# Alternating the products of two score or value blocks in a decoder layer's attention

## Chip, cores and metric

The kernel runs on one core of one Trainium2 chip. The metric is the device time of one execution in microseconds (us); 0.2% of it is 5 us.

## The reference, cut to what matters

One decoder layer on x (2 batches, 512 tokens, 1024 features), float32:

```python
q = (x @ w_q)   # 32 heads of 128;  k, v = x @ w_k, x @ w_v   # 8 heads of 128
lq = x @ w_lq   # 256 wide;  lk = lq @ w_lk, lv = x @ w_lv    # 32 heads of 128
q, k, lk = rope(q), rope(k), rope(lk)
attn = causal_attn(q, k, v);  lat = causal_attn(q, lk, lv)
x = layernorm(x + attn @ w_o + lat @ w_lo)
x = layernorm(x + fake_quant(x) @ fake_quant(ctx))
x = layernorm(x + fp8_simulated(x) @ weight)
```

causal_attn is softmax(mask(q k^T / sqrt(128))) v.

## The kernel before, in words

**Split products.** Every float32 operand of a large product is split into a high part and a low part, both fp32r. `product` (L1198) makes one product of three matmuls into the same PSUM tile: high by high (L1200), high by the moving low part (L1201), low by high (L1202). The first name is the stationary operand, which a weight load puts into the array before each matmul; the profile lists these loads as engine PEld, with the same line as their matmul.

**Groups.** For each of 2 batches there are 8 groups, one per key and value head, so 16 in all. A group G computes, in this order on TensorE: lk from lq, the values of the group before's last unit, k and v, q, lv (each from weight chunks of 128x512 that SP loads, ScalarE copies to w_hi at L478 and GpSimd turns into w_lo at L414), and then 8 units of attention: 4 query heads with k, v and the same 4 with lk, lv. lv lands in the four banks BANK_B; ScalarE copies each to lv_hi (L658), VectorE subtracts to lv_lo (L962) and counts `lv_lo_done`.

**A unit** has three steps on TensorE. `scores(G, u)` (L1211) makes the lower triangle of the 512x512 scores in four blocks, one per tile of 128 queries, with 512, 384, 128 and 256 keys, in the order of the table `TRI`; they lie in banks 0, 1, 1 and 2. Each block is one `product`, and counts `scores_ready`. VectorE's `mask_scores` (L801, its instructions at L809) masks the blocks and takes a row minimum in the order of `TRI`; it waits for 1, 3, 3 and 4 counts. ScalarE makes exponentials (L515), VectorE normalises (L816, L820). `transposes(G, u)` (L1235, L1248) waits for the masks of unit u + 1 and for the normalised rows of unit u, and transposes ten 128x128 tiles into banks 0 to 2. ScalarE copies them to pT_hi (L521), VectorE makes pT_lo (L826). `values(G, u)` (L1253) multiplies by v or lv in four blocks by key tile, 512, 384, 256 and 128 queries wide (`sorted(PT)`), all accumulated in bank 3 (columns 128*kt to 512), and counts `o_ready`. ScalarE and VectorE take it to o_hi (L525) and o_lo (L831).

**Order around it.** The order is written out by hand (L1435 to L1447): part 0, scores 0, part 1, scores 1, and then for each u: part, transposes u, part, values u, scores u + 2. A part is one chunk of the output projection, 12 matmuls 512 wide, added up by VectorE at L845. In a steady group part(0) lies between the lv products and scores 0; in the first group of batch 0 there is nothing there.

At unit 0, `scores` waits for lv_lo before it overwrites the banks: the block in bank 0 for the first lv_lo of the group, the one in bank 1 for the second, the one in bank 2 for the third. Everything else that scores and values wait for is waited for once, ahead of their first matmul.

Of the kernel before, what the change touches and what calls it, by code (L numbers as in the profile page):

```python
# [14 lines left out]
P = 128  # L15
B, S, D = 2, 512, 1024
H, KVH, HD = 32, 8, 128
# [5 lines left out]
TT = S // P  # L23
N = 512
# [30 lines left out]
TRI = [(3, 0, 0, 512), (2, 1, 512, 384), (0, 1, 896, 128), (1, 2, 1024, 256)]  # L55
PT = [(0, 0, 0, 512), (1, 1, 512, 384), (3, 1, 896, 128), (2, 2, 1024, 256)]
SPW = 1280
PT_BANKS = [(0, 0, 512), (1, 512, 512), (2, 1024, 256)]


# [35 lines left out]
def program(nc, wstream, xt, x, ctxt, wf, cos, sin, mask, ident, quant, out):  # L96
    ctx = ExitStack()
    with ctx:
        def sem(name):
            return ctx.enter_context(nc.semaphore(name))  # L100
# [11 lines left out]
        def sb(name, shape, dt, stack=ctx):  # L112
            return stack.enter_context(nc.sbuf_tensor(name, shape, dt))
# [19 lines left out]
        with ExitStack() as mem:  # L133
            xT_hi, xT_lo = (sb(n, [P, KT, S], F32R, mem) for n in ("xT_hi", "xT_lo"))
            lq_hi, lq_lo = (sb(n, [P, 2, S], F32R, mem) for n in ("lq_hi", "lq_lo"))
            k_hi, k_lo = (sb(n, [P, S], F32R, mem) for n in ("k_hi", "k_lo"))
            v_hi, v_lo = (sb(n, [P, TT, HD], F32R, mem) for n in ("v_hi", "v_lo"))
            q_hi, q_lo = (sb(n, [P, HG, S], F32R, mem) for n in ("q_hi", "q_lo"))
            lk_hi, lk_lo = (sb(n, [P, HG, S], F32R, mem) for n in ("lk_hi", "lk_lo"))
            lv_hi, lv_lo = (sb(n, [P, TT, HG * HD], F32R, mem) for n in ("lv_hi", "lv_lo"))  # L140
            probs = sb("probs", [P, 2, SPW], F32, mem)
            pT_hi, pT_lo = (sb(n, [P, SPW], F32R, mem) for n in ("pT_hi", "pT_lo"))
            acc = sb("acc", [P, TT, D], F32, mem)
# [51 lines left out]
        BANK_B = [ctx.enter_context(nc.psum_tensor(f"bank_b{i}", [P, N], F32)) for i in range(4)]  # L195
# [22 lines left out]
        lv_hi_done, lv_lo_done = sem("lv_hi_done"), sem("lv_lo_done")  # L218
        scores_ready = sem("scores_ready")
# [249 lines left out]
        def _(act):  # L469
# [48 lines left out]
            def pT_high(G, u):  # L518
                for i, (bank, at, w) in enumerate(PT_BANKS):
                    act.wait_ge(pT_ready, 3 * (UNITS * G + u) + i + 1)  # L520
                    nc.scalar.activation(pT_hi[:, at:at + w], BANK_B[bank][:, 0:w], ACT.Copy).then_inc(pT_hi_done, 1)  # L521
# [260 lines left out]
        def _(dve):  # L782
# [40 lines left out]
            def pT_low(G, u):  # L823
                for i, (bank, at, w) in enumerate(PT_BANKS):
                    dve.wait_ge(pT_hi_done, 3 * (UNITS * G + u) + i + 1)
                    nc.vector.tensor_tensor(pT_lo[:, at:at + w], BANK_B[bank][:, 0:w],  # L826
                                            pT_hi[:, at:at + w].bitcast(F32), ALU.subtract).then_inc(pT_lo_done, 1)
# [368 lines left out]
        def _(pe):  # L1196
            def product(dst, still, move, start, stop):


                nc.tensor.matmul(dst, still[0], move[0], start=start, stop=False)  # L1200
                nc.tensor.matmul(dst, still[0], move[1], start=False, stop=False)  # L1201
                return nc.tensor.matmul(dst, still[1], move[0], start=False, stop=stop)  # L1202

            def weights(pos, a, z):
                s = SPLIT_SLOT[pos]
                return w_hi[:, s, a:z], w_lo[:, s, a:z]

            def xk(k, a=0, z=S):
                return xT_hi[:, k, a:z], xT_lo[:, k, a:z]

            def scores(G, u):  # L1211

                h = 2 * (u // 4) + u % 2
                if u == 0:

                    pe.wait_ge(rope_lo, ROPES * G + ROPES)
                elif u == 1:

                    pe.wait_ge(masked, 4 * (UNITS * G + 1))
                else:  # L1220

                    pe.wait_ge(pT_lo_done, 3 * (UNITS * G + u - 1))
                for i, (qt, bank, at, w) in enumerate(TRI):
                    q = q_hi[:, h, P * qt:P * qt + P], q_lo[:, h, P * qt:P * qt + P]
                    if u % 4 < 2:
                        k = k_hi[:, 0:w], k_lo[:, 0:w]
                    else:
                        k = lk_hi[:, h, 0:w], lk_lo[:, h, 0:w]
                    col = at - N * bank
                    if u == 0 and i != 2:  # L1230

                        pe.wait_ge(lv_lo_done, TT * G + bank + 1)
                    product(BANK_B[bank][:, col:col + w], q, k, True, True).then_inc(scores_ready, 1)

            def transposes(G, u):  # L1235

# [16 lines left out]
            def values(G, u):  # L1253

                h = 2 * (u // 4) + u % 2
                pe.wait_ge(pT_lo_done, 3 * (UNITS * G + u + 1))
                if u == 0:

                    pe.wait_ge(v_lo_done, G + 1)
                    pe.wait_ge(lv_lo_done, TT * G + TT)  # L1260
                else:

                    pe.wait_ge(o_lo_done, UNITS * G + u)
                for kt, _, at, w in sorted(PT):
                    if u % 4 < 2:
                        v = v_hi[:, kt], v_lo[:, kt]
                    else:
                        v = lv_hi[:, kt, HD * h:HD * (h + 1)], lv_lo[:, kt, HD * h:HD * (h + 1)]
                    p = pT_hi[:, at:at + w], pT_lo[:, at:at + w]
                    last = product(BANK_B[3][:, P * kt:N], v, p, kt == 0, kt == TT - 1)  # L1270
                last.then_inc(o_ready, 1)

            def split(b, g, c):
# [56 lines left out]
            def group(b, g, first):  # L1330
# [15 lines left out]
                if not first:  # L1346

                    values(G - 1, UNITS - 1)
# [85 lines left out]

                part(0)  # L1435
                scores(G, 0)
                part(1)
                scores(G, 1)
                for u in range(UNITS):
                    if u < UNITS - 1:  # L1440
                        part(2 * u + 2)
                    transposes(G, u)
                    if u < UNITS - 1:
                        part(2 * u + 3)
                        values(G, u)
                    if u + 2 < UNITS:
                        scores(G, u + 2)  # L1447
# [6 lines left out]
            for b in range(B):  # L1454

                for c in range(C_LQ):
                    split(b, 0, c - C_LQ)
                    for k in (2 * c, 2 * c + 1):
# [3 lines left out]
                        for l in range(2):  # L1462
                            if k == 0 and b:

                                pe.wait_ge(added, 4 * (4 * KVH * b - 1) + l + 1)
                            at = LAT * (k % 2) + P * l
                            last = product(BANK_A[l][:], weights(LQ_POS + c, at, at + P), xk(k),
                                           k == 0, k == KT - 1)
# [13 lines left out]
                for i in range(C_TAIL // 2):  # L1482
                    if i == 2:
                        values(KVH * (b + 1) - 1, UNITS - 1)
                    if i in (0, 3):

                        pe.wait_ge(o_lo_done, UNITS * KVH * (b + 1) - (0 if i else 1))
                    last_output(b, i)
# [155 lines left out]
```

## Time and profile before

| | |
|---|---|
| median of 3 runs | 2533.32 us (2532.18 to 2535.01) |
| profiled execution, own time | 2531.58 us |
| its span | 2529.6 us |
| TensorE busy | 2468.4 us, 98% of the span |
| matmuls, weight loads | 12456 and 12456 |
| VectorE, ScalarE, GpSimd busy | 69%, 45%, 36% |
| mean granted clock | 0.994 |

PE is TensorE's matmuls, PEld its weight loads, DVE VectorE, ACT ScalarE, POOL GpSimd. The span is shorter than the execution's own time by what lies around the program. Matmuls are pipelined, so the duration of one is longer than the distance to the next.

### The profile page before, as it was taken

Reading aid. Unit: us, or ns where it says so; the run is one execution under the profiler, and the core shown is the slowest. Engines: PE = TensorE matmul, PEld = TensorE weight load, DVE = VectorE, ACT = ScalarE, POOL = GpSimd, SP = SyncE. Lnnn points to the kernel's source line nnn. Section 1 sums busy time; section 2 is a strip of 40 time slices with the busy share of each in tenths; the row PEclk is TensorE's granted clock in tenths of the full one; section 3 lists DMA queues with packets and bytes.
Section 4 is the critical chain, followed back from the end, with each engine's and each line's share of the span. In section 5 each row is a group of like instructions: output and inputs, shape, how many; then the busy total and the mean of one; then the engine's idle time right before and its main releaser. Section 6 shows DMA issues by size and latency. Waiting matters only on the chain.

```text
span 2529.6 us, 40729 instructions
## 1 busy us (share of the span) xinstructions
PE 2468.4 (98%) x12456; PEld 2088.7 (83%) x12456; DVE 1734.9 (69%) x3589; ACT 1131.9 (45%) x2576; POOL 921.8 (36%) x696
## 2 busy tenths in 40 slices
PE   7899999999999999999989999999999999999998
PEld 6688888888888888887767888888888888888877
DVE  5676767767676767665587676767767677667656
ACT  3444434344444535444365453544444354544551
POOL 4334242433434242432543424243342524334210
PEclk9999999999999999999999999999999999999999
DMA  5323231312223232322423323222232323234411
GB/s 179 89 80 92 64 104 58 98 56 75 87 75 95 62 98 60 90 64 87 136 89 131 105 70 109 69 85 77 83 104 71 109 70 106 60 90 147 154 34 67
DMA packets 124407, 226.26 MB, mean 89 GB/s; under 512 B 13088, under 2 KB 21408, under 8 KB 124192
## 3 DMA queue, kind: packets, MB, share of 16 engines
q1 hardware_dynamic: 119552, 216.91, 28.2%
q10 hardware_dynamic: 4768, 8.39, 0.9%
q8 instruction: 30, 0.49, 0.1%
q14 instruction: 57, 0.47, 0.1%
HBM read 206.37 MB, written 18.87 MB: 89 GB/s over the span
## 4 chain that ended last, share of the span: by engine, by line
PE 94%; DVE 3%; issue 1%; ACT 1%; DMA 0%; POOL 0%; SPq 0%; PEldq 0%; ACTq 0%; DVEq 0%
PE bank_a L1200 16%; PE bank_a L1202 16%; PE bank_a L1201 16%; PE bank_b L1200 13%; PE bank_b L1201 13%; PE bank_b L1202 13%; PE bank_b L1248 5%; PE bank_b L1517 1%; PE bank_a L1325 0%; DMA probs<-xt 0%; DVE probs L809 0%; PE bank_b L1384 0%; PE bank_b L1500 0%; POOL w_lo L414 0%; DVE acc L845 0%
## 5 line engine op out<-in xcount | busy, mean ns | idle before, releaser
L414 POOL TENSOR_TENSOR w_lo<-w_raw,w_hi 128x512 fp32r<-128x512 f32 x632 | 844.0, 1344 | 1419.2 <-ACT w_hi L478 1411.2
L478 ACT ACTIVATE w_hi<-w_raw 128x512 fp32r<-128x512 f32 x632 | 392.9, 626 | 287.9 <-DMA w_raw<-wstream 141.5
L1200 PE MATMUL bank_a<-w_hi,o_hi 128*128 128x512 f32 x1024 | 410.7, 401 | 9.0 <-DVE acc L845 4.8
L1202 PE MATMUL bank_a<-w_hi,o_lo 128*128 128x512 f32 x1024 | 403.5, 394 | 0.0
L1201 PE MATMUL bank_a<-w_lo,o_hi 128*128 128x512 f32 x1024 | 403.1, 394 | 0.0
L826 DVE TENSOR_TENSOR pT_lo<-bank_b,pT_hi 128x512 fp32r<-128x512 f32 (+1 forms) x384 | 207.0, 594 | 267.1 <-ACT pT_hi L521 267.1
L515 ACT ACTIVATE probs<-probs,row_min 128x512 f32<-128x512 f32 (+3 forms) x512 | 281.6, 552 | 240.8 <-DVE row_min L809 238.4
L525 ACT ACTIVATE o_hi<-bank_b 128x512 fp32r<-128x512 f32 x128 | 76.8, 600 | 455.4 <-PE bank_b L1202 455.4
L820 DVE TENSOR_SCALAR probs<-probs,row_inv 128x512 f32<-128x512 f32 (+3 forms) x512 | 261.4, 570 | 4.5
L1200 PEld LDWEIGHTS bank_a<-w_hi,o_hi 128*128 128x128 f32 x1024 | 193.5, 189 | 44.3 <-issue 7.8
L1200 PE MATMUL bank_a<-xT_hi,w_hi 128*128 128x512 f32 x544 | 214.2, 394 | 14.4 <-POOL w_lo L414 14.4
L1202 PEld LDWEIGHTS bank_a<-w_hi,o_lo 128*128 128x128 f32 x1024 | 193.1, 189 | 41.7
L1201 PEld LDWEIGHTS bank_a<-w_lo,o_hi 128*128 128x128 f32 x1024 | 193.6, 189 | 34.9
L809 DVE CUSTOM_DVE_ANT_0 probs<-bank_b,mask_sb 128x512 f32<-128x512 f32 (+3 forms) x512 | 220.5, 482 | 2.4 <-PE bank_b L1202 1.0
L1202 PE MATMUL bank_a<-xT_hi,w_lo 128*128 128x512 f32 x544 | 212.8, 391 | 0.0
L1201 PE MATMUL bank_a<-xT_lo,w_hi 128*128 128x512 f32 x544 | 212.7, 391 | 0.0
L1200 PE MATMUL bank_b<-w_hi,xT_hi 128*128 128x512 f32 x512 | 199.2, 389 | 0.0
L1201 PE MATMUL bank_b<-w_lo,xT_hi 128*128 128x512 f32 x512 | 199.2, 389 | 0.0
L1202 PE MATMUL bank_b<-w_hi,xT_lo 128*128 128x512 f32 x512 | 199.2, 389 | 0.0
L790 DVE TENSOR_TENSOR probs<-bank_a,cos_sb 128x512 f32<-128x512 f32 x128 | 88.2, 689 | 136.5 <-PE bank_a L1202 130.5
L521 ACT ACTIVATE pT_hi<-bank_b 128x512 fp32r<-128x512 f32 (+1 forms) x384 | 171.6, 518 | 18.1 <-PE bank_b L1248 18.1
L1248 PE MATMUL bank_b<-ident_sb,probs 128*128 128x128 f32 x1280 | 162.3, 274 | 11.7 <-DVE row_min L809 10.9
(176 smaller groups left out, 4785.4 us busy)
## 6 DMA issues: line engine op xcount, KB each, us to landing
w_raw<-wstream SPq DMA_DIRECT2D x632, 256.0 KB, 2.7
stage<-ctx SPq DMA_DIRECT2D x32, 256.0 KB, 2.7
stage_w<-wf SPq DMA_DIRECT2D x32, 256.0 KB, 2.8
q_scratch<-stage_q SPq DMA_DIRECT2D x32, 128.0 KB, 2.3
wf_hi_scratch<-piece_hi SPq DMA_DIRECT2D x16, 256.0 KB, 3.0
wf_lo_scratch<-stage_w SPq DMA_DIRECT2D x16, 256.0 KB, 3.3
wf_hi<-wf_hi_scratch SPq DMA_DIRECT2D x8, 512.0 KB, 7.9
wf_lo<-wf_lo_scratch SPq DMA_DIRECT2D x8, 512.0 KB, 11.8
```

The costliest lines, as they stand in the source:

```text
L414: nc.gpsimd.tensor_tensor(w_lo[:, s], w_raw[:, r], w_hi[:, s].bitcast(F32), ALU.subtract).then_inc(lo_done, 1)
L478: nc.scalar.activation(w_hi[:, s], w_raw[:, r], ACT.Copy).then_inc(hi_done, 1)
L515: nc.scalar.activation(part, part, ACT.Exp, bias=row_min[:, u % 2, i:i + 1], scale=-1.0, accum_out=row_sum[:, u % 2, i:i + 1]).then_inc(ex ...
L521: nc.scalar.activation(pT_hi[:, at:at + w], BANK_B[bank][:, 0:w], ACT.Copy).then_inc(pT_hi_done, 1)
L790: nc.vector.tensor_tensor(a, bank[:], cos_sb[:], ALU.mult)
L809: nc.vector.tensor_tensor_reduce(out=probs[:, u % 2, at:at + w], in0=BANK_B[bank][:, col:col + w], in1=mask_sb[:, N - w:N], scale=-SCALE, ...
L820: nc.vector.tensor_scalar(part, part, row_inv[:, u % 2, i:i + 1], None, ALU.mult).then_inc(normed, 1)
L826: nc.vector.tensor_tensor(pT_lo[:, at:at + w], BANK_B[bank][:, 0:w], pT_hi[:, at:at + w].bitcast(F32), ALU.subtract).then_inc(pT_lo_done, 1)
L1200: nc.tensor.matmul(dst, still[0], move[0], start=start, stop=False)
L1201: nc.tensor.matmul(dst, still[0], move[1], start=False, stop=False)
L1202: return nc.tensor.matmul(dst, still[1], move[0], start=False, stop=stop)
L1248: last = nc.tensor.transpose(BANK_B[bank][:, dst:dst + P], probs[:, u % 2, src:src + P], ident_sb[:])
```

## The change

The blocks of scores and values are taken in two pairs: the first table row with the third, the second with the fourth. In both tables these are 512 with 128 columns, and 384 with 256. Within a pair the loops run over the three parts of the product outside and the two blocks inside. The operands, the sums and the number of matmuls stay. Scores of unit 0 wait once per pair for the lv_lo of the pair's second block; values start their accumulation at block 0, part 0, and end it with the last part of the last block.

```diff
+TRI_PAIRS = [(0, 2), (1, 3)]
+PT_PAIRS = [(0, 2), (1, 3)]
...
-                for i, (qt, bank, at, w) in enumerate(TRI):
-                    q = q_hi[:, h, P * qt:P * qt + P], q_lo[:, h, P * qt:P * qt + P]
-                    if u % 4 < 2:
-                        k = k_hi[:, 0:w], k_lo[:, 0:w]
-                    else:
-                        k = lk_hi[:, h, 0:w], lk_lo[:, h, 0:w]
-                    col = at - N * bank
-                    if u == 0 and i != 2:
-
-                        pe.wait_ge(lv_lo_done, TT * G + bank + 1)
-                    product(BANK_B[bank][:, col:col + w], q, k, True, True).then_inc(scores_ready, 1)
+                for pair in TRI_PAIRS:
+                    if u == 0:
+
+                        pe.wait_ge(lv_lo_done, TT * G + TRI[pair[1]][1] + 1)
+                    for part in range(3):
+                        for i in pair:
+                            qt, bank, at, w = TRI[i]
+                            q = (q_lo if part == 2 else q_hi)[:, h, P * qt:P * qt + P]
+                            if u % 4 < 2:
+                                k = (k_lo if part == 1 else k_hi)[:, 0:w]
+                            else:
+                                k = (lk_lo if part == 1 else lk_hi)[:, h, 0:w]
+                            col = at - N * bank
+                            last = nc.tensor.matmul(BANK_B[bank][:, col:col + w], q, k, start=part == 0, stop=part == 2)
+                            if part == 2:
+                                last.then_inc(scores_ready, 1)
...
-                for kt, _, at, w in sorted(PT):
-                    if u % 4 < 2:
-                        v = v_hi[:, kt], v_lo[:, kt]
-                    else:
-                        v = lv_hi[:, kt, HD * h:HD * (h + 1)], lv_lo[:, kt, HD * h:HD * (h + 1)]
-                    p = pT_hi[:, at:at + w], pT_lo[:, at:at + w]
-                    last = product(BANK_B[3][:, P * kt:N], v, p, kt == 0, kt == TT - 1)
+                for pair in PT_PAIRS:
+                    for part in range(3):
+                        for i in pair:
+                            kt, _, at, w = PT[i]
+                            if u % 4 < 2:
+                                v = (v_lo if part == 2 else v_hi)[:, kt]
+                            else:
+                                v = (lv_lo if part == 2 else lv_hi)[:, kt, HD * h:HD * (h + 1)]
+                            p = (pT_lo if part == 1 else pT_hi)[:, at:at + w]
+                            first, stop = (kt, part) == (0, 0), (pair, part, i) == (PT_PAIRS[-1], 2, pair[1])
+                            last = nc.tensor.matmul(BANK_B[3][:, P * kt:N], v, p, start=first, stop=stop)
                 last.then_inc(o_ready, 1)
```

## Rows read from the trace of the kernel before

**Rows 1.** The page: busy time, and the chain that ended last, by engine.
```profile
PE 2468.4 (98%) x12456; PEld 2088.7 (83%) x12456; DVE 1734.9 (69%) x3589; ACT 1131.9 (45%) x2576; POOL 921.8 (36%) x696
...
PE 94%; DVE 3%; issue 1%; ACT 1%; DMA 0%; POOL 0%; SPq 0%; PEldq 0%; ACTq 0%; DVEq 0%
```
**Rows 2.** Stretch table of one steady group: busy us, granted clock, DMA share, GB/s.
```profile
960.14:1103.85 143.71, 143.71 (x734) 122.97 (x733) 99.94 (x210) 64.42 (x153) 52.83 (x40) 1.00 0.27 79
```
**Rows 3.** Waits of TensorE, whole span: total us, times, longest us.
```profile
PE bank_b L1200 <- DVE lv_lo L962: 6.5, 1, 6.5
```
**Rows 4.** Timeline of loads and one matmul, values then scores: start us, duration us.
```profile
1005.54 0.19 PEld L1201 LDWEIGHTS bank_b<-pT_lo,v_hi 128*128 128x128 f32 x1
...
1005.54 0.39 PE L1200 MATMUL bank_b<-pT_hi,v_hi 128*128 128x512 f32 x1
...
1005.77 0.19 PEld L1202 LDWEIGHTS bank_b<-pT_hi,v_lo 128*128 128x128 f32 x1
...
1006.22 0.19 PEld L1201 LDWEIGHTS bank_b<-pT_lo,v_hi 128*128 128x128 f32 x1
...
1007.12 0.19 PEld L1201 LDWEIGHTS bank_b<-pT_lo,v_hi 128*128 128x128 f32 x1
1007.22 0.19 PEld L1202 LDWEIGHTS bank_b<-pT_hi,v_lo 128*128 128x128 f32 x1
...
1007.45 0.19 PEld L1201 LDWEIGHTS bank_b<-lk_lo,q_hi 128*128 128x128 f32 x1
...
1008.14 0.19 PEld L1201 LDWEIGHTS bank_b<-lk_lo,q_hi 128*128 128x128 f32 x1
...
1008.49 0.19 PEld L1200 LDWEIGHTS bank_b<-lk_hi,q_hi 128*128 128x128 f32 x1
1008.66 0.19 PEld L1201 LDWEIGHTS bank_b<-lk_lo,q_hi 128*128 128x128 f32 x1
1008.77 0.19 PEld L1202 LDWEIGHTS bank_b<-lk_hi,q_lo 128*128 128x128 f32 x1
...
1009.00 0.19 PEld L1201 LDWEIGHTS bank_b<-lk_lo,q_hi 128*128 128x128 f32 x1
...
1009.36 0.19 PEld L1201 LDWEIGHTS bank_a<-w_lo,o_hi 128*128 128x128 f32 x1
```
**Rows 5.** Matmuls by form, 970 to 1028 us: busy us, mean ns of one.
```profile
L1200 PE MATMUL bank_b<-pT_hi,v_hi 128*128 128x512 f32 x3 | 1.2, 389 | 0.0
...
L1202 PE MATMUL bank_b<-pT_hi,v_lo 128*128 128x384 f32 x3 | 1.0, 339 | 0.0
...
L1200 PE MATMUL bank_b<-pT_hi,v_hi 128*128 128x256 f32 x3 | 0.9, 290 | 0.0
...
L1201 PE MATMUL bank_b<-pT_lo,v_hi 128*128 128x256 f32 x3 | 0.8, 282 | 0.0
...
L1200 PE MATMUL bank_b<-pT_hi,v_hi 128*128 128x128 f32 x3 | 0.7, 220 | 0.0
```
**Rows 6.** Timeline where scores of unit 0 begin: a steady group, then group 0.
```profile
1093.02 2.48 DVE L962 TENSOR_TENSOR lv_lo<-bank_b,lv_hi 128x512 fp32r<-128x512 f32 x4 [6.50 <-ACT lv_hi L658]
...
1094.17 0.19 PEld L1200 LDWEIGHTS bank_b<-k_hi,q_hi 128*128 128x128 f32 x1
...
87.90 2.48 DVE L962 TENSOR_TENSOR lv_lo<-bank_b,lv_hi 128x512 fp32r<-128x512 f32 x4 [6.05 <-ACT lv_hi L658]
88.71 0.19 PEld L1200 LDWEIGHTS bank_b<-k_hi,q_hi 128*128 128x128 f32 x1 [2.48 <-issue]
```
**Rows 7.** Timeline: last mask row of a unit, and the transposes that wait for it.
```profile
1011.19 0.08 DVE L809 DVE_READ_ACCUMULATOR2_ANT row_min<- 128x1 f32 x1
...
1012.11 0.27 PE L1248 MATMUL bank_b<-ident_sb,probs 128*128 128x128 f32 x1
...
1102.58 0.07 DVE L809 DVE_READ_ACCUMULATOR2_ANT row_min<- 128x1 f32 x1
...
1103.69 0.38 PE L1248 MATMUL bank_b<-ident_sb,probs 128*128 128x128 f32 x2
```

## The prediction

> **What bounds the kernel now.** I read the page's first part and the chain that ended last: TensorE is busy for 98% of the span, holds 94% of the chain, at nearly full granted clock [rows 1]. The stretch table of one steady group, of which 14 of the 16 are alike, shows TensorE busy for all of its 143.71 us at a granted clock of 1.00, 2.4 GHz, with VectorE at 99.94 us [rows 2]. The waits of TensorE, third, are single events in the first group of a batch: the one of this change's place is 6.5 us, once [rows 3]. So whatever changes the time between two matmuls is paid in full, and what shifts on other engines is paid only once a wait appears.
>
> The fourth view, the weight loads in order of time, prices a matmul [rows 4]. A load starts when the matmul before it starts to stream: the load and the matmul of 1005.54 have one start. So the gap between two loads is what one matmul costs. 512 columns cost 0.23 us (1005.54 to 1005.77), 384 cost 0.17 (1008.14 to 1008.66 for three), 256 cost 0.12 (1009.00 to 1009.36), and 128 cost 0.11: the three narrow ones of the values stream from 1007.12 and the next 512 from 1007.45. Durations are finer [rows 5]: a 512 lasts 389 ns and costs 227, so I take 162 off a duration (my choice of constant) where the matmul waited for no load. The first narrow one of the values streams in 220 - 162 = 58 ns, yet the next one starts 0.11 later. A narrow product is bound by the load that follows it.
>
> **The change part by part.** Its intent can only be to hide that load: 110 - 58 = 52 ns for each of 3 narrow products, in 128 scores and 128 values.
>
> First, *the alternation itself*. Which matmul has the long gap? The load for the second narrow product of the scores starts at 1008.66, when the first one starts to stream, though the 384 before it streams from 1008.49 and the load during that one began at 1008.49 too; the load after it comes 0.11 later (1008.77), which is all that a load needs [rows 4]. Had a second load been allowed to run ahead, it would have begun about 1008.60. It didn't, and the wide rows say the same: 0.23 between loads that need 0.11. One load runs ahead, never two. Then in 512, 128, 512 the load of the second 512 can only start as the 128 starts, and the 512 waits for it: 0.23 + 0.11, as now. Each pair costs what its members cost apart; the narrow matmul merely has another neighbour. Number of loads and matmuls: unchanged. Taken: 0. That product now gives q_hi or v_hi twice running is no credit lost either: loads are issued again for each of the three parts [rows 4], and the second matmul of a product, with the same stationary operand, has its load at 1005.54 like any other.
>
> The Trainium skill ("TensorE: Matmul & The Clock Gate", section "Step-by-step: what each phase is for") says that TensorE's 64-deep window pulls weight loads ahead of matmuls in flight when they go to the background buffer. Read as many loads ahead, it would give the first rival below; the trace agrees only with one load ahead.
>
> Second, *changes of width*. They carry small surcharges [rows 5]. The last 384 lasts 339 ns and the 256 after it 290, so 177 + 128 = 305 ns for a 384 with a 256 behind it; a 256 behind a 256 costs 282 - 162 = 120. The new order has such a pair three times: 915 ns. The values take 0.90 us for these six (1006.22 to 1007.12), the scores 0.52 for the 384s and 0.36 for the 256s, 0.88 [rows 4]. That is 15 + 35 = 50 ns a unit. For the 512 and 128 pairs the rows show 0.23 and 0.11 whatever stands before (1007.45 follows a narrow one by 0.11), taken as 0. So 50 x 128 units = 6.4 us. Bounds: below, every surcharge vanishes, 3 x 227 + 520 + 3 x 120 + 330 = 1891 ns against 1.91 us, in values (1005.54 to 1007.45) and in scores (1007.45 to 1009.36), 0.02 x 256 sets = -5.1 us. Above, width changes within a set go from 3 to 11, and each of the 8 more costs the 8 ns by which 290 lies over 282: 64 x 256 = +16.4 us. Whether the surcharge stays when the order alternates no row shows; I take the pair that exists.
>
> Third, *the earlier wait at unit 0*. Before, the first scores product waits for the first lv_lo and the second for the second; now the pair waits for the second at once. VectorE's four lv_lo of a steady group run from 1093.02 for 2.48 us, 0.62 each: the first two end at 1093.64 and 1094.26. The first scores load starts at 1094.17 [rows 6]. In group 0 the load started at 88.71 after the first lv_lo, which by the same count ended at 88.52: 0.19 later. So in the changed kernel the load starts at 1094.45, and streaming follows 0.11 behind, as behind every load that is waited for, at 1094.56. Now it follows a load that was early, with the end of the 512 before it, 0.23 behind the load, at 1094.40. The difference is 0.16 us, and the bound TensorE doesn't get it back. 14 x 0.16 = 2.2 us. In the first group of each batch TensorE already waits for the first lv_lo (load at 88.71, and the 6.5 us of the second batch) [rows 3, 6], so it waits one lv_lo longer, 0.6 each: 1.2 us. Bounds: 0 if the release is quicker and the two late ones absorb theirs, 4 us if the later masks of the two first groups add up. The third lv_lo, at 1094.9, is there before the second pair's loads near 1095.5: no cost.
>
> Fourth, *later readiness of the scores*. The first tile is ready after 5 matmuls instead of 3, at 0.9 instead of 0.7 us from the start; the second mask, which waits for three, can go after 11 instead of 9, about 0.25 later. In the unit loop VectorE ends the masks of the scores of 1007.45 at 1011.27, and the transposes that need them start at 1012.11 [rows 7]: slack 0.84 us, over three times the delay. Behind unit 0 the masks may end 0.45 later; those of unit 1, out at 1102.65, are then out near 1103.1, against transposes at 1103.69 [rows 7]. Queued behind a late mask are the exponentials and, behind them on ScalarE, a w_hi made four chunks ahead. Cost 0; if the cover is gone, whatever exceeds it, once per unit. No DMA, no instruction of SP or POOL moves.
>
> **Sum.** 0 + 6.4 + 2.2 + 1.2 = +9.8 us on the profiled execution's 2531.58 us (span 2529.6 and 2 around it): 2541.4. The median of the runs shown is 1.7 above that execution; on it the forecast is 2543.1.
>
> **Rivals.**
> *Two or more loads run ahead.* Then a wide matmul of 227 ns nearly hides the load of both neighbours (two loads, 220), a narrow one costs about 58, and 52 x 768 = 39.9 us are saved, less 3.4 of waiting: about 2496.8. For it: only that loads are separate instructions that overlap matmuls. Against: every load start in rows 4. This is the case on the other side.
> *No surcharge.* The alternating order costs no more than blocks do, or a little less; the waits remain. -2 to +5 us, about 2535, no change that shows. For it: the 282 and 290 differ for no reason that I can give, so it may be a phase and not a price.
> *The masks become the wait.* If the masks ended over 0.84 us later, TensorE would stand before the transposes in each. At 0.2 us beyond the slack, 0.2 x 128 = 26 us more: about 2568. Against: I count 0.25.
> *The change doesn't alternate.* Were the matmuls issued in another order than written, nothing would move but the waits. They follow the code's order in every row I read; I give this nothing of its own.
>
> **Chances.** Forecast 0.58; no surcharge 0.30; two loads ahead 0.07; masks 0.05. About 0.2%, 5 us, is what a measurement of this kernel can tell from no change. The forecast's spread reaches from +5 to +19, so nearly all of it is slower; a little falls inside, and of the no-surcharge case all but a sliver is inside. Faster 0.08, same 0.32, slower 0.60. The range takes the low ends together, -5.1 + 1.8 if the waits are absorbed in part, to 2530, and the high ends, 16.4 + 4 = 20.4, less a little because both at their worst is unlikely, to 2552; the two outer rivals are left out, with 0.12, and a little for what I haven't seen.
>
> **What would show it.** Right: after each 128 the next load starts 0.11 behind the load before, and a 512 behind it starts to stream only then; a set of 12 takes 1.92 to 1.94 us; the first scores product of a steady group starts at 0.1 to 0.2 us of idle after lv_lo; TensorE's counts stay at 12456. Wrong: load starts 0.06 apart anywhere in the pairs (two ahead), a set near 1.75 us; or waits of the transposes for the masks in the unit loop; or a 256 behind a 384 that lasts 282 ns, which takes the surcharge away.

## The result, and the profile after

The changed kernel takes 2538.72 us (median of 15 runs, 2536.42 to 2541.33) against 2533.15 us beside it: a ratio of 1.0021, 95% interval 1.0013 to 1.0028, which is +5.3 us with +3.3 to +7.1. Forecast were +9.8 us, between 2530 and 2552. The direction and the range held; the sum was nearly twice too large, and its two leading terms were sized wrong in the same direction. A piece that no term named, the clock, fills part of the gap, so that the number came as near as it did is in part luck.

The stretch table of one steady group of the changed kernel, to be read beside [rows 2]:

```profile
962.86:1106.71 143.85, 143.85 (x735) 122.67 (x734) 100.15 (x210) 64.48 (x152) 52.81 (x40) 1.00 0.28 79
```

A group grows from 143.71 to 143.85 us (143.82 to 143.87 in all but one of the 48 distances read). TensorE is still busy throughout: what is lost lies inside the matmuls' distances. The twelve distances from one steady group's first lk product to the next one's, six in each batch, sum to 1724.6 us before (mean of three profiles) and 1726.1 after (mean of four): +1.5 us, or some 1.7 for all 14 steady groups.

The weight loads in order of time, for the values and scores that answer to [rows 4]. A row "x2" holds the loads of one part of a pair, and its start is that of the first. In these rows the stationary operand, the one that is loaded, is the second name behind the arrow:

```profile
1008.52 0.30 PEld L1282 LDWEIGHTS bank_b<-pT_lo,v_hi 128*128 128x128 f32 x2
1008.86 0.30 PEld L1282 LDWEIGHTS bank_b<-pT_hi,v_lo 128*128 128x128 f32 x2
1009.20 0.30 PEld L1282 LDWEIGHTS bank_b<-pT_hi,v_hi 128*128 128x128 f32 x2
1009.49 0.31 PEld L1282 LDWEIGHTS bank_b<-pT_lo,v_hi 128*128 128x128 f32 x2
1009.78 0.30 PEld L1282 LDWEIGHTS bank_b<-pT_hi,v_lo 128*128 128x128 f32 x2
1010.08 0.30 PEld L1239 LDWEIGHTS bank_b<-lk_hi,q_hi 128*128 128x128 f32 x2
1010.43 0.30 PEld L1239 LDWEIGHTS bank_b<-lk_lo,q_hi 128*128 128x128 f32 x2
```

A pair of 512 and 128 takes 0.34 us (1008.52 to 1008.86): 0.23 + 0.11, the sum of what the two cost apart. A pair of 384 and 256 takes 0.29. Nothing was hidden. The durations say where the wait went. The forms of the matmuls, mean ns of one, for [rows 5]:

```profile
L1282 PE MATMUL bank_b<-pT_lo,v_hi 128*128 128x512 f32 x3 | 1.3, 445 | 0.0
...
L1282 PE MATMUL bank_b<-pT_hi,v_lo 128*128 128x384 f32 x3 | 1.0, 340 | 0.0
...
L1282 PE MATMUL bank_b<-pT_lo,v_hi 128*128 128x256 f32 x3 | 0.8, 278 | 0.0
...
L1282 PE MATMUL bank_b<-pT_lo,v_hi 128*128 128x128 f32 x3 | 0.7, 222 | 0.0
```

In the kernel before, the second and third narrow matmul of a set lasted about 275 ns, waiting some 55 ns of it for their own load:

```profile
L1201 PE MATMUL bank_b<-pT_lo,v_hi 128*128 128x128 f32 x3 | 0.8, 276 | 0.0
```

Now each lasts 222, and the 512 behind it lasts 445 instead of 389: the same wait, moved to the neighbour. A reader who looked at the narrow rows alone would see a gain of a fifth.

The earlier wait of unit 0, first in a steady group (for [rows 6]), then the whole span's row for [rows 3]:

```profile
1095.73 2.48 DVE L965 TENSOR_TENSOR lv_lo<-bank_b,lv_hi 128x512 fp32r<-128x512 f32 x4 [6.50 <-ACT lv_hi L661]
...
1097.07 0.30 PEld L1239 LDWEIGHTS bank_b<-k_hi,q_hi 128*128 128x128 f32 x2 [0.23 <-DVE lv_lo L965]
```
```profile
PE bank_b L1239 <- DVE lv_lo L965: 9.7, 2, 7.0
```

The first scores load now waits for the second lv_lo. It starts 1.34 us after the first lv_lo began, where it started 1.15 after (1093.02 to 1094.17). In the first group of a batch the matmul's wait is 7.0 instead of 6.5 us, and there are two such groups in the list instead of one.

The piece that no term named is the clock. Around the tail, rows of the stretch table (after PE, PEld, DVE, ACT and POOL comes the granted clock), the kernel before first, then the changed one:

```profile
2424.00:2428.00 4.00, 1.76 (x19) 1.21 (x18) 3.97 (x5) 3.30 (x6) 2.17 (x1) 1.00 0.00 0
2428.00:2432.00 4.00, 4.00 (x19) 3.25 (x19) 3.72 (x4) 3.97 (x6) 2.60 (x2) 1.00 0.00 0
```
```profile
2431.00:2434.00 3.00, 0.76 (x14) 0.59 (x12) 2.96 (x4) 2.48 (x5) 1.85 (x1) 1.00 0.00 0
2434.00:2438.00 4.00, 4.00 (x15) 3.19 (x13) 3.90 (x4) 4.00 (x4) 2.89 (x2) 0.57 0.00 0
```

TensorE sits idle for over 2 us in both. In the kernel before it goes on at 2.4 GHz (granted 1.00); in the changed one the next stretch is granted 0.57, mostly 1.2 GHz, and issues 15 matmuls in place of 19. From the last group's lk products to the end the changed kernel takes 292.9 us instead of 291.1: 1.8 us, of which the steady group in it makes about 0.1 and the clock 1.6 to 1.7.

### The profile page after: what moved, and what is told of

The parts are those of the page before. It is cut to its first block, busy times and chain, and to the rows that moved or that the text cites. A ratio compares the mean times of both kernels' runs of the same rounds, so it can differ in the third digit from the quotient of the medians.

```text
span 2537.5 us, 40715 instructions
## 1 busy us (share of the span) xinstructions
PE 2472.9 (97%) x12456; PEld 2085.4 (82%) x12456; DVE 1736.9 (68%) x3589; ACT 1132.1 (45%) x2576; POOL 923.0 (36%) x696
## 4 chain that ended last, share of the span: by engine, by line
PE 94%; DVE 3%; issue 2%; ACT 1%; DMA 0%; POOL 0%; SPq 0%; PEldq 0%; ACTq 0%; DVEq 0%; POOLq 0%
PE bank_a L1203 16%; PE bank_a L1204 16%; PE bank_a L1205 16%; PE bank_b L1282 10%; PE bank_b L1239 9%; PE bank_b L1204 7%; PE bank_b L1203 7%; PE bank_b L1205 7%; PE bank_b L1256 5%; PE bank_a L1337 1%; PE bank_b L1529 1%; POOL w_lo L417 0%; DVE probs L812 0%; DMA probs<-xt 0%; PE bank_b L1396 0%
## 5 line engine op out<-in xcount | busy, mean ns | idle before, releaser
L1256 PE MATMUL bank_b<-ident_sb,probs 128*128 128x128 f32 x1280 | 161.7, 273 | 12.6 <-DVE row_min L812 11.8
## 6 DMA issues: line engine op xcount, KB each, us to landing
wf_lo<-wf_lo_scratch SPq DMA_DIRECT2D x8, 512.0 KB, 11.8
```

Source lines behind the costliest of these rows:

```text
L1256: last = nc.tensor.transpose(BANK_B[bank][:, dst:dst + P], probs[:, u % 2, src:src + P], ident_sb[:])
```

## The experiments

All ratios are against the kernel before, run in turn on the same chip.

**Theory.** One load runs ahead, so alternation is neutral but for some ns; the loss comes from the earlier wait. **Rivals.** The alternation costs it; or loads run further ahead and something else eats the gain.

**e1: the wait alone**

```diff
-                        pe.wait_ge(lv_lo_done, TT * G + bank + 1)
+                        pe.wait_ge(lv_lo_done, TT * G + max(bank, 1) + 1)
```

> The kernel before, with only the wait moved: scores of unit 0 wait for the second lv_lo ahead of the first block. No alternation. My theory (waits and the rest of the scores order are separate costs): the first scores load of a steady group starts 0.11 to 0.12 us after the second lv_lo ends, streaming 0.14 us later than before, 14 x 0.14 = 2.0 us, and 0.6 us in each first group: +3.2 us. Rival (the cost of the change is in the alternation): 0 to +1 us.

Measured 1.0015 (1.0006 to 1.0024), +3.8 us, interval +1.5 to +6.1. So the wait alone makes a loss, by the middle value most of it. But its steady groups grow less than expected:

```profile
741.60:885.40 143.80, 143.80 (x736) 122.89 (x733) 100.27 (x211) 64.30 (x152) 52.37 (x40) 1.00 0.26 79
```

0.09 a group, 1.3 us in all, and the scores of each first group start 0.6 later: 2.5. In its profile the tail has the slow clock too, worth 1.7, though nothing alternates:

```profile
2428.00:2432.00 4.00, 4.00 (x16) 3.21 (x14) 3.90 (x4) 3.99 (x4) 2.95 (x2) 0.57 0.00 0
```

**e2: both alternations, with the waits put back**

```diff
-                    if u == 0:
-                        pe.wait_ge(lv_lo_done, TT * G + TRI[pair[1]][1] + 1)
                     for part in range(3):
                         for i in pair:
                             qt, bank, at, w = TRI[i]
+                            if u == 0 and part == 0 and i != 1:
+                                pe.wait_ge(lv_lo_done, TT * G + bank + 1)
```

> The changed kernel with the waits of the kernel before put back: the first matmul waits for the first lv_lo, the narrow one behind it for the second, the last block for the third. My theory: the narrow product's load in a steady group waits 0.04 us instead of 0.14, so 1.4 us of the 2.0 come back and up to 0.2 in each first group: 1.5 to 2.5 us less than the changed kernel, about +3 us against before. Rival (alternation costs it all): still +5 us.

Measured 1.0013 (1.0004 to 1.0022), +3.3 us. Steady group and the first group's start behave as expected: the group takes 143.74 us, 0.03 over the kernel before, and the first group's scores start when they did.

```profile
740.76:884.50 143.74, 143.74 (x734) 122.72 (x733) 100.22 (x212) 64.30 (x152) 52.37 (x40) 1.00 0.26 79
```

The tail's clock stays up (291.3 us from the last group's lk to the end). The total agrees with the number expected, but its interval reaches from +1.0 to +5.6 and doesn't exclude the rival, so the group time is the evidence here, not the total. Of the +3.3 only 0.4 to 0.5 lies in the steady groups. Its profile has another fall of the clock, near 1210 us, worth 1.6 (see e9 to e12); what is left isn't placed.

**e3 and e4: one alternation each.** e3 has the scores of the changed kernel and the values of the kernel before, e4 the reverse:

```diff
-                for pair in PT_PAIRS:
...
+                for kt, _, at, w in sorted(PT):
...
```
```diff
-                for kt, _, at, w in sorted(PT):
...
+                for pair in PT_PAIRS:
...
```

> Only the scores alternate, with the change's wait. From the loads of the changed kernel: a set of scores takes 1920 ns instead of 1913, so 128 x 7 ns = +0.9 us, and the waits +3.2: about +4.1 us. Rival (values carry the loss): under +2 us.

> Only the values alternate. A set of values takes 1903 ns instead of 1904 in the changed kernel: 0 us, within the noise, though its 512s cost 7 ns more each and its 256s 8 ns less. My prediction's surcharge of 15 ns a set would give +1.9 us; the rival that a second load runs ahead would give -20 us.

e3: 1.0023 (1.0014 to 1.0032), +5.8 us, where +4.1 was expected: that number left out the tail's fall, which e3's profile has. e4: 0.9999 (0.999 to 1.0008), no change. Steady groups, e3 then e4:

```profile
741.39:885.22 143.83, 143.83 (x734) 122.72 (x733) 100.34 (x212) 64.29 (x152) 52.38 (x40) 1.00 0.27 79
```
```profile
739.93:883.59 143.66, 143.66 (x734) 122.88 (x733) 100.17 (x212) 64.32 (x152) 52.46 (x40) 1.00 0.26 79
```

e3 over e1 is the scores' alternation without the wait: 0.03 a group. e4 under the kernel before is the values': -0.05 a group. Added up they would give 14 x (0.03 - 0.05) = -0.3 us. Both together, read directly as the changed kernel over e1, which has the same wait, give 1726.1 against 1725.8 us over the twelve distances: +0.03 a group, +0.4 us in all. Either way alternation costs next to nothing in the steady groups, where I had 6.4.

**e5: a larger dose of the wait**

```diff
-                        pe.wait_ge(lv_lo_done, TT * G + bank + 1)
+                        pe.wait_ge(lv_lo_done, TT * G + TT)
```

> The kernel before, with every block of unit 0 waiting for the fourth lv_lo: a larger dose of the wait. In a steady group the fourth ends 1.34 us after the first load's time; with 0.11 to the load and 0.11 to streaming less the 0.23 that the load was ahead: +1.33 us x 14 = 18.7 us, and 1.8 us in each first group: +22 us. Rival (the wait is absorbed behind it): clearly less, under +10 us.

Measured 1.0089 (1.0075 to 1.0103), +22.5 us, and a group of 145.00 with 1.00 us of TensorE idle:

```profile
893.90:1038.90 145.00, 144.00 (x736) 122.89 (x733) 100.02 (x211) 64.41 (x152) 52.76 (x40) 1.00 0.26 78
```

1.29 a group: a steady group pays the wait in full.

**e6: narrow matmuls halved in the changed order**

```diff
+                            n = w if w > P else w // 2
-                            last = nc.tensor.matmul(BANK_B[bank][:, col:col + w], q, k, ...
+                            last = nc.tensor.matmul(BANK_B[bank][:, col:col + n], q, k[:, 0:n], ...
```

and the same in values.

> The changed kernel with every 128-wide matmul of scores and values cut to 64 columns; half of the diagonal block of the first 128 queries and of the last key block is left out of the computation. My theory (a narrow matmul is bound by the load behind it, which needs 0.11 us, whatever its neighbours): no change against the changed kernel, +5 us against before, load gaps still 108 ns. Rival (alternation has hidden the load and narrow matmuls cost their streaming): 768 x 27 ns = 20 us less.

Measured 1.0005 (0.9996 to 1.0014), +1.3 us: 4 us under the changed kernel, not 0, but far from 20. By form:

```profile
L1284 PE MATMUL bank_b<-pT_lo,v_hi 128*128 128x512 f32 x4 | 1.9, 476 | 0.0
...
L1284 PE MATMUL bank_b<-pT_lo,v_hi 128*128 128x64 f32 x4 | 0.8, 193 | 0.0
```
```profile
1006.23 0.30 PEld L1284 LDWEIGHTS bank_b<-pT_lo,v_hi 128*128 128x128 f32 x2
1006.57 0.30 PEld L1284 LDWEIGHTS bank_b<-pT_hi,v_lo 128*128 128x128 f32 x2
1006.91 0.30 PEld L1284 LDWEIGHTS bank_b<-pT_hi,v_hi 128*128 128x128 f32 x2
```

The narrow matmul is 29 ns shorter and the 512 behind it 31 ns longer; the pair still takes 0.34 us. This puts the rival of a hidden load out: even with half its columns gone a narrow product costs the 0.11 of the load behind it, next to the widest block. Of the 4 us, 1.6 are the tail's clock, which stays up here (291.3 us to the end), and about 1.2 smaller distances elsewhere in the sets (groups of 143.74). The last us I can't place; it is less than the interval.

e6 shows that the columns don't set the 0.11, but not yet that the load does: every matmul here has a load, so a fixed price per matmul would look alike. e5's trace settles that. There TensorE has been idle for 1.00 us when the scores of unit 0 begin:

```profile
960.16 0.19 PEld L1200 LDWEIGHTS bank_b<-k_hi,q_hi 128*128 128x128 f32 x1 [1.43 <-DVE lv_lo L962]
960.16 0.50 PE L1200 MATMUL bank_b<-k_hi,q_hi 128*128 128x512 f32 x1 [1.00 <-DVE lv_lo L962]
960.27 0.19 PEld L1201 LDWEIGHTS bank_b<-k_lo,q_hi 128*128 128x128 f32 x1
```

With no matmul ahead of it, the first load still takes 0.108 to 0.109 us until the next one starts, in all 14 steady groups, and its matmul lasts 0.50 us, 0.11 more than the 0.39 of a 512 that waits for nothing. The load alone needs the 0.11. It isn't the price of every load: the bf16 loads of the kernel before, 0.10 us long, come 0.055 us apart (seven of them end 0.43 us after the first one's start).

```profile
2440.69 0.43 PEld L1312 LDWEIGHTS bank_b<-ident_b,q 128*128 128x128 bf16 x7
```

**e7: other partners, values only**

```diff
-PT_PAIRS = [(0, 2), (1, 3)]
+PT_PAIRS = [(0, 3), (1, 2)]
```

> Only the values alternate, with other partners: 512 with 256, and 384 with 128. My theory (a pair costs what its members cost apart, plus some ns of surcharge): within 1 us of e4, sets of 1.90 us; the 128 costs 0.108 behind a 384 as behind a 512. Rival (what matters is that the widest covers the narrowest): slower than e4 by 2 us or more.

Measured 1.0009 (1.0 to 1.0018), +2.3 us, with groups of 143.81 against e4's 143.66:

```profile
740.86:884.67 143.81, 143.81 (x734) 122.97 (x733) 99.94 (x212) 64.39 (x152) 52.83 (x40) 1.00 0.27 79
```

My number missed, and the rival's fits. Its mechanism doesn't: the 128s last 221 to 222 ns, and the 384s behind them 391 to 397 instead of 339, the same transfer of the wait as behind a 512. What differs are some ns elsewhere: here a 512 behind a 256 lasts 395 to 403.

```profile
L1276 PE MATMUL bank_b<-pT_hi,v_lo 128*128 128x512 f32 x4 | 1.6, 403 | 0.0
L1276 PE MATMUL bank_b<-pT_lo,v_hi 128*128 128x384 f32 x4 | 1.6, 397 | 0.0
...
L1276 PE MATMUL bank_b<-pT_hi,v_hi 128*128 128x128 f32 x4 | 0.9, 222 | 0.0
```

So such surcharges are real, 0.15 us a group or 18 ns a unit, but I can't tell their sign from the neighbours' widths. More than half of them even lies in the scores, whose order e7 leaves as it was: their 384 with k_lo or lk_lo lasts 342 to 346 ns instead of 337 to 338. The total isn't evidence for the rival either: e4 and e7 ran beside different runs of the kernel before, and e7's profile has the fall near 1210 us, worth 1.6, that e4's hasn't.

**e8: the change again**, beside e5 to e7.

> The changed kernel as it is, beside these on one chip. Expected +5.3 us as measured, 3 to 7; of it the waits make about 3 and the sets 0.7.

Measured 1.0021 (1.0012 to 1.003), +5.3 us, as before.

**e9 to e12: is the clock's fall one of the kernel or of the execution?** Both kernels unchanged, twice each.

> The kernel before, unchanged, profiled again. In its first profile the clock stayed at 2.4 GHz near 1210 us and near 2430 us; in the changed kernel's two profiles there is a stretch of 3.4 us at 1.2 GHz at each, worth 1.6 and 1.7 us. Theory A (the clock's falls there differ from execution to execution and belong to no kernel): this profile or the next shows at least one such stretch. Theory B (they belong to the shifted waits of the changed kernel): neither shows one.

> As the run before it: the kernel before, unchanged. Theory A: its pattern of half-clock stretches differs from the other profiles of the same kernel. Theory B: it is the first profile's pattern, none near 1210 and 2430 us.

> The changed kernel, unchanged, profiled again. Theory A: at least one of the two stretches at 1.2 GHz (near 1212 and 2430 us) is missing here or in the next run. Theory B: both are there in both runs, as in its two profiles so far.

> As the run before it: the changed kernel, unchanged. In every profile of it the steady groups are expected at 143.82 to 143.86 us, the set of scores at 1920 ns and the set of values at 1903 ns, whatever the clock does in the stretches between.

The two places answer differently. Near 1210 us, in the second batch's lq products, the fall is in one of three profiles of the kernel before and in all four of the changed one; a fall there is worth 1.6 us (15.6 instead of 14.0 from the first lq product to lk). Of the other kernels' profiles, one each, e2, e3, e5, e6 and e7 have it, e1 and e4 don't. e10 has it:

```profile
1211.00:1215.00 4.00, 4.00 (x12) 3.14 (x11) 0.00 (x0) 1.04 (x2) 4.00 (x4) 0.57 0.78 234
2428.00:2432.00 4.00, 1.76 (x19) 1.33 (x18) 3.93 (x5) 3.30 (x6) 2.37 (x1) 1.00 0.00 0
2432.00:2436.00 4.00, 4.00 (x19) 3.28 (x18) 3.47 (x3) 3.96 (x6) 2.41 (x1) 1.00 0.00 0
```

In the tail it is in none of the three before, and in all four after, as e12 shows:

```profile
2432.00:2436.00 4.00, 4.00 (x17) 3.22 (x15) 3.90 (x4) 3.97 (x5) 2.98 (x2) 0.57 0.00 0
```

So theory A holds near 1210, where it can happen to either kernel, and B as far as seven profiles can say for the tail. Of the other kernels, by one profile each, the tail's fall is in e1 and e3, not in e2, e4, e5, e6 and e7. e6 has the changed order and the pair's wait and doesn't show it; e5 has the longest wait and doesn't either. The idle ahead of it, 2.46 us between the starts of two matmuls, is the same in all. So no single edit brings it; that small shifts in time decide it is my guess, and how they would I leave open.

The mean granted clocks of all executions bear on this as well. They are 0.9937 and 0.9936 in the kernel before (33 and 27 executions) and 0.9928 and 0.9927 in the changed one (15 and 11): 0.0009 less, which over 2535 us is about 2 us of lost work if it all fell into TensorE's working time. So the changed kernel loses more to the clock in its other executions too. In e1 the mean over 11 executions is 0.9936, as before; that the tail's fall is part of e1's +3.8 rests on its one profile.

The steady groups repeat as e12's expectation says: 143.83 to 143.86 in it.

## Why the prediction was right, and where it was not

*The alternation hides nothing* (taken: 0). Right, and shown by the loads of the changed kernel and by e6: one load runs ahead, and a load for the matmul after a narrow one starts only with the narrow one. The rival of two or more loads ahead is out: 0.34 us a pair, where it needed 0.29 or less (227 + 58 ns). The Trainium skill's sentence in "TensorE: Matmul & The Clock Gate" ("Step-by-step: what each phase is for") that loads are pulled ahead holds here with one load and no more.

*Changes of width* (taken: +6.4 us). Wrong: between -0.3 and +0.4 us measured in the steady groups, by e3 and e4 or by the changed kernel over e1. This is the step that made the sum too large. It took "the pair that exists", a 384 of 177 ns with a 256 of 128 behind it, and multiplied it by three. In the alternation the 256 costs 278 - 162 = 116 ns, no more than the cheapest before, and the 384 176 to 180; the pair is 295, not 305. The prediction named this sign of being wrong itself: a 256 behind a 384 that lasts 282 ns; it lasts 278 to 281. The 512 and 128 pairs, taken at 0, became dearer instead: a 512 behind a narrow one costs 445 - 389 = 56 more in its duration, of which 53 are the wait, and 233 to 240 where it was 227 to 232. The two nearly cancel: a set of values takes 1903 instead of 1904 ns, a set of scores 1920 instead of 1913 (sums of the median distances between loads), 6 ns a unit where the prediction had 50. My "no surcharge" rival, 0.30, was the better account of this term, though its number for the whole was too low. The neighbour rows of one order don't price another one to 10 ns.

*The wait in steady groups* (2.2 us). Right in kind, about half in size: 1.3 by e1. The step that failed is the lag of 0.19 between the end of lv_lo and the load, from group 0, and the even share of 0.62 for each lv_lo. The first lv_lo of group 0 lasts 0.69, so the lag there is 0.12, and in a steady group it is 0.05. There the load starts 1.34 after the first lv_lo begins, not 1.43; with streaming 0.11 behind it that is 1.45, against 1.15 + 0.22 = 1.37 before, which gives the 0.09 of e1.

*The wait in the two first groups* (1.2 us). Right: in both the scores start 1.4 us after the first lv_lo begins instead of 0.8, and the two groups take 0.5 and 0.7 us longer.

*Later readiness of the scores* (0). Right for the steady groups, not quite for the first ones. The transposes' wait for masks stays with single events:

```profile
PE bank_b L1256 <- DVE row_min L812: 11.8, 8, 3.1
```

These are 8 events as before, all in first groups, but 0.9 us more in sum:

```profile
PE bank_b L1248 <- DVE row_min L809: 10.9, 8, 3.3
```

The sum varies with the longest of the 8, which is either about 3.2 or about 1.4 us. Among profiles alike in that, it is 0.9 to 1.5 us larger wherever the scores alternate: 11.8 (e2 and three profiles of the changed kernel) against 10.9, and 10.1 to 10.3 (e3, e6, e12) against 8.8 to 9.1 (e1, e4, e5, e7, e10). So the alternation's later scores do delay the masks where nothing covers them. It doesn't show in the total: the two first groups together grow by 1.2 us, which is what the lv_lo wait makes.

*What no term named.* The tail runs on the slow clock in all four profiles. By stretches, as means of three profiles before and four after, in us:

| stretch | before | changed | difference |
|---|---|---|---|
| start to the first lk | 26.5 | 26.4 | -0.1 |
| first group of batch 0 | 141.1 | 141.6 | +0.5 |
| twelve steady groups | 1724.6 | 1726.1 | +1.5 |
| steady group 7 and all up to batch 1's first lk | 194.0 | 195.0 | +1.0 |
| first group of batch 1 | 153.7 | 154.4 | +0.7 |
| last steady group and tail | 291.1 | 292.9 | +1.8 |
| span | 2531.1 | 2536.3 | +5.3 |

The +1.0 is the fall near 1210 us, met in 4 of 4 against 1 of 3 profiles at 1.6 each; whether that is chance is open. So of the 5.3 about 2.9 belong to the change's waits and its alternation (1.7 in the steady groups, 1.2 in the first ones), and 2.4 to the clock, of which the prediction had nothing.

## What to carry to other kernels

When narrow fp32r matmuls cost more than they stream, look at which load they are bound by: if the gap between two load starts never falls under that of one load, order can't hide it, and what could gain is fewer or wider matmuls, or operands whose load is shorter, as the bf16 one is here (0.055 us against 0.11); none of these was tried. A matmul that got shorter may have handed its wait to the next: judge by the distance over the whole pair, not by the mean of one form. And when a loop is interleaved, look at which waits were hoisted ahead of the first product; here that cost more than the reordering itself, and e2 shows that putting them where each block needs them takes 0.11 of the 0.14 us a steady group back. The whole times of e2 and the changed kernel, +3.3 and +5.3, don't part them beyond their intervals. No version here beats the kernel before: e4, the best, is equal to it.

## What the runs showed that I had not expected

The clock can differ far from any edit: in e1 only a wait was changed, by a tenth of a microsecond a group, and in its profile the tail, some 2300 us later than the first of them, ran at a granted clock of 0.57 for one stretch after an idle that both kernels have. That the wait is the cause isn't shown, since e5, with a longer wait, doesn't have it. And partners in an alternation differ by 18 ns a unit (e7 against e4) with the same matmuls and the same number of loads.
